# Mixture of experts with a router: slots turned into rows by one-hot products, and gathers and scatters moved into the expert stage

## The reference

```python
xn = (x - mu) * jax.lax.rsqrt(var + EPS) * gamma + beta          # 6250 x 256
logits = jnp.einsum('bsd,de->bse', xn, Wr) + br                  # 8 experts
top_vals, top_idx = jax.lax.top_k(logits, K)                     # K = 2
w = jax.nn.softmax(top_vals, axis=-1)
...
for e in range(E):
    h = jax.nn.gelu(jnp.einsum('bsd,dh->bsh', xn, W1[e]) + b1[e], approximate=False)   # 256 -> 512
    y_e = jnp.einsum('bsh,hd->bsd', h, W2[e]) + b2[e]                                  # 512 -> 256
    y = y + y_e * w_full[..., e, None]
```

## Time and profile before

| | us |
|---|---|
| median of 3 runs | 4773.51 |
| lowest and highest run | 4771.86, 4778.14 |
| the profiled execution | 4775.09 |
| its span, first to last instruction | 4773.1 |

### The profile page before, as it was taken

The page is one execution under the profiler, slowest core; times in us unless marked ns, Lnnn a source line. Parts: engine busy times, 40 slices in busy tenths (PEclk is TensorE's granted clock), DMA queues, the critical chain, the costliest instruction groups (busy, mean ns, idle before and its releaser), DMA issues. The chain is left out here.

```text
span 4773.1 us, 64840 instructions
## 1 busy us (share of the span) xinstructions
PE 3211.2 (67%) x14347; PEld 2378.1 (50%) x14348; DVE 2956.0 (62%) x7184; ACT 2137.5 (45%) x5151; POOL 2786.5 (58%) x2929
## 2 busy tenths in 40 slices
PE   4367777777756677777779477777777450499970
PEld 1255555555545455555569365656565340266640
DVE  5677777777757777777754577777777771022223
ACT  0444434444433344444434477777777450133321
POOL 0277776776657767777746577777777356100016
PEclk9988888888878888888889689898988655699995
DMA  2434333333323333333322111111111613411115
GB/s 85 135 111 116 116 114 109 110 110 110 106 87 109 106 96 109 111 110 110 111 63 72 35 34 35 34 35 34 35 33 33 133 50 124 158 55 55 55 62 144
DMA packets 266610, 411.78 MB, mean 86 GB/s; under 512 B 77798, under 2 KB 183427, under 8 KB 266052
## 3 DMA queue, kind: packets, MB, share of 16 engines
q0 software_dynamic: 120320, 275.83, 22.7%
q1 hardware_dynamic: 145988, 132.65, 8.7%
HBM read 325.12 MB, written 83.11 MB: 86 GB/s over the span
## 5 line engine op out<-in xcount | busy, mean ns | idle before, releaser
L1482 PE MATMUL conv_ps<-conv_msg,conv_S 128*128 128x256 f32 x3328 | 1073.3, 472 | 405.9 <-DVE ACC L1492 310.8
L1482 PEld LDWEIGHTS conv_ps<-conv_msg,conv_S 128*128 128x128 f32 x3328 | 742.3, 236 | 652.7 <-DVE ACC L1492 308.3
L1458 POOL DMA_INDIRECT conv_msg<-relu_xn_table,GI x832 | 787.8, 947 | 387.6 <-issue 247.4
L1458 POOL DMA_INDIRECT conv_msg<-conv_table,GI x832 | 794.5, 955 | 326.5 <-issue 249.6
L2326 POOL DMA_INDIRECT gat_msg<-attn_table,GI x832 | 824.6, 991 | 266.2 <-issue 253.3
L1492 DVE TENSOR_TENSOR ACC<-ACC,conv_ps 128x256 f32 x1664 | 700.7, 421 | 417.1 <-issue 245.7
L1467 ACT ACTIVATE conv_S<-iota_row,LOC 128x128 f32<-128x128 f32 x1664 | 507.3, 388 | 538.2 <-PE conv_ps L1482 529.9
L2383 PE MATMUL gat_ps<-gat_M,gat_S 128*128 128x260 f32 x1664 | 506.7, 458 | 106.4 <-DVE gat_M L2484 102.2
L2383 PEld LDWEIGHTS gat_ps<-gat_M,gat_S 128*128 128x128 f32 x1664 | 364.0, 227 | 185.2 <-DVE gat_M L2484 117.1
L3001 POOL DMA_INDIRECT combine_y<-expert_out,combine_at x98 | 94.1, 960 | 579.7 <-ACTq L2989 559.9
L2441 DVE TENSOR_TENSOR ACC<-ACC,gat_ps 128x260 f32 x832 | 349.0, 419 | 33.9 <-PE gat_ps L2383 11.3
(11 more groups left out here) (535 smaller groups left out, 5625.3 us busy)
## 6 DMA issues: line engine op xcount, KB each, us to landing
expert_in<-heads_zrow SPq DMA_DIRECT2D x53, 256.0 KB
experts_xe<-expert_in SPq DMA_DIRECT2D x106, 128.0 KB
expert_out<-experts_y SPq DMA_DIRECT2D x106, 128.0 KB, 1.7
conv_msg<-relu_xn_table,GI POOLq DMA_INDIRECT x832, 2.8
conv_msg<-conv_table,GI POOLq DMA_INDIRECT x832, 2.8
gat_msg<-attn_table,GI POOLq DMA_INDIRECT x832, 2.5
relu_xn_table<-begin_rx SPq DMA_DIRECT2D x49, 128.0 KB, 1.7
xnT<-begin_xt SPq DMA_DIRECT2D x49, 128.0 KB, 1.8
```

The costliest lines, as they stand in the source:

```text
L1458: pool.indirect_dma_start(self.msg[:, h * RING + k, :], None, table, bass.IndirectOffsetOnAxis(ap=self.m.GI[:, t:t + 1], axis=0)).then_inc ...
L1482: self.nc.tensor.matmul(self.ps[k % self.NB][:, 0:D], self.S[:, r % 2, k, :], self.msg[:, r % self.DEEP * RING + k, :], start=True, stop=T ...
```

## The change

1. **Gamma and beta move behind the transposes.** They are loaded once, at the program's start, as one number per partition (`m.gammac`, `m.betac`, [128, 2]). What PE transposes and SP stores is now the bare `xn`. In heads, ACT's two activations with scale and bias stand where one copy stood, and POOL has nothing to do. In experts, DVE scales the transposed tile with two tensor_scalar operations where ACT copied it.
2. **`expert_in`, its zeros and the dispatch stage are gone.** At the end of route the places are inverted: for each expert tile and slot, which choice (1 to 12,500 and a few) stands there. Each of 98 columns of places gives a one-hot of its slot (`places`, 128 wide) and a one-hot of its tile (`tiles`, 106 wide), which ACT multiplies by the choice's number (`numbered`); PE adds up the 98 products in one PSUM tile. DVE makes them seven columns at a time, 14 rounds, three in flight. A little arithmetic turns the sum into `from_row` (which row of `m.xm` to read) and `to_row` (where in a DRAM tensor `answers` to write).
3. **The experts gather and send.** POOL gathers the 128 rows of each tile from `m.xm` by `from_row` and scatters the answers by `to_row`; SP has no part in the stage. PE's transposes of tile t+1 stand behind tile t's W1 product.
4. **Combine reads plainly.** Answers lie in node order, first all first choices, then all second ones. SP loads them four tiles at a time (two DMAs of 512 KB), DVE does eight operations with one drain, ACT stores 512 KB. Four such parts are in flight, 13 parts in all.
5. **The weights are loaded during route**, from the stage's first moment.

```diff
@@ stage_load
-            for to, frm in ((m.b11s, m.b11), (m.b21s, m.b21)):
+            for to, frm in ((m.b11s, m.b11), (m.b21s, m.b21), (m.gammac, m.gamma), (m.betac, m.beta)):
@@ stage_heads_to_router, scalar
                     if i >= TS:
-                        act.wait_ge(u_made, i - TS + 1)
-                    nc.scalar.activation(t[:, i % TS, :], x_of(i), ACT.Identity, scale=m.rstd[:, i:i + 1],
-                                         bias=shift[:, i:i + 1]).then_inc(t_made, 1)
+                        act.wait_ge(turned, i - TS + 1)
+                        act.wait_ge(out_xn[i % TS], i // TS * 16)
+                    nc.scalar.activation(xn[:, i % TS, :], x_of(i), ACT.Identity, scale=m.rstd[:, i:i + 1],
+                                         bias=shift[:, i:i + 1]).then_inc(xn_made, 1)
...
-                    nc.scalar.copy(xt[:, i % TS, :], pt[i % 2][:, 0:D]).then_inc(xt_made, 1)
+                    for c in range(2):
+                        op = nc.scalar.activation(xt[:, i % TS, c * P:c * P + P], pt[i % 2][:, c * P:c * P + P], ACT.Identity,
+                                                  scale=m.gammac[:, c:c + 1], bias=m.betac[:, c:c + 1])
+                    op.then_inc(xt_made, 1)
@@ stage_route, vector
+            for g in range(CHOICES // SEVEN):
+                if g >= RINGS:
+                    v.wait_ge(placed, g - RINGS + 1)
+                for hot, frm, w in ((places, low, P), (tiles, high, EX_TILES)):
+                    op = nc.vector.tensor_tensor(hot[:, g % RINGS, :, :], m.iota_row[:, 0:w].unsqueeze(1).broadcast_to([P, SEVEN, w]),
+                                                 frm[:, g * SEVEN:(g + 1) * SEVEN].unsqueeze(2).broadcast_to([P, SEVEN, w]), ALU.is_equal)
+                op.then_inc(one_hots, 1)
@@ stage_route, scalar and tensor
+                for k in range(SEVEN):
+                    n = g * SEVEN + k
+                    op = nc.scalar.activation(numbered[:, g % RINGS, k, :], tiles[:, g % RINGS, k, :], ACT.Copy, scale=number[:, n:n + 1])
+                op.then_inc(numbers, 1)
...
+                for k in range(SEVEN):
+                    n = g * SEVEN + k
+                    mm = nc.tensor.matmul(inverse[:, 0:EX_TILES], places[:, g % RINGS, k, :], numbered[:, g % RINGS, k, :],
+                                          start=(n == 0), stop=(n == CHOICES - 1))
+                mm.then_inc(placed, 1)
@@ stage_experts
+        @block.gpsimd
+        def _(pool):
+            for t in range(EX_TILES + BEHIND):
+                if t < EX_TILES:
+                    if t >= 2:
+                        pool.wait_ge(turned, t - 1)
+                    pool.indirect_dma_start(xe[t % 2][:, :], None, m.xm,
+                                            bass.IndirectOffsetOnAxis(ap=m.from_row[:, t:t + 1], axis=0)).then_inc(x_in[t % 2], 16)
+                u = t - BEHIND
+                if u >= 0:
+                    pool.wait_ge(y_made, u + 1)
+                    pool.indirect_dma_start(m.answers, bass.IndirectOffsetOnAxis(ap=m.to_row[:, u:u + 1], axis=0),
+                                            y[u % 2][:, :], None).then_inc(stored[u % 2], 16)
@@ stage_experts, vector
+            def scaled(t, s):
+                v.wait_ge(turned, t + 1)
...
+                for c in range(2):
+                    op = nc.vector.tensor_scalar(xt[s][:, c * P:c * P + P], pt[s][:, c * P:c * P + P], m.gammac[:, c:c + 1],
+                                                 m.betac[:, c:c + 1], ALU.mult, ALU.add)
+                op.then_inc(xt_made, 1)
@@ stage_combine, sync
+            for j, (lo, n, rows) in enumerate(parts):
+                if j >= RINGS:
+                    sp.wait_ge(out_made, j - RINGS + 1)
+                for k in range(2):
+                    sp.dma_start(y[j % RINGS][0:rows, k * FOUR:k * FOUR + n, :],
+                                 rows_of(m.answers, k * TILES + lo, n, rows)).then_inc(got[j % RINGS], 16)
```

283 lines of the change are left out of this document (119 added, 164 removed).

## The result

| | before | after |
|---|---|---|
| median | 4775.16 us (4771.86 to 4778.14) | 4515.93 us (4514.64 to 4520.99, 4 runs) |
| profiled execution's span | 4773.1 us | 4519.3 us |
| ratio of the medians | | 0.9459, 95% interval 0.9443 to 0.9476 |

What follows compares the result with a forecast made beforehand. POOL's indirect DMAs were taken to bound dispatch and combine, PE's wait ahead of W1 the experts, stretched DVE operations heads. Terms +1 - 18 - 118.5 - 38.6 - 67.3 = -241.4 gave 4532 us, range 4505 to 4578.

Steps and rivals of the forecast that it cites:

- Start: Program start: two more small loads in SP's list, ahead of the load of x, cost +1 us.
- Heads: Heads stage: POOL's 98 operations and DVE's stretching go, ACT is late next; -18 us, ends -5 and -25.
- 65.5 + 15 = 81 us: Heads: ACT's busy time plus 15 us for two activations over 35 tiles, as ACT's floor; 82 taken for 100.2.
- Route and dispatch: Last place to experts' start: 158.3 us go, 39.8 us of inversion, small steps and barrier come; -118.5 us.
- The rule on the clock: Inversion on TensorE: small idle gaps make its clock swing, so rounds would cost between 35 and 52 us.
- Experts: Expert stage: period 4.756 to 4.37 us over 106 tiles, -41, ends dearer by 0.8 and 1.5; sum -38.6 us.
- rival A: Experts: the loop through bias and Gelu keeps the period at 4.756 us; 4573 us in all, chance 0.14.
- Combine: Combine stage: plain loads replace 98 gathers and small copies, 69 us for 136.3; -67.3 us, ends -78 and -54.
- B: TensorE stays at 1.2 GHz in the inversion, or combine's DMAs run at 282 GB/s; +17, +13, both 4562; chance 0.13.
- E: Weights written during route slow DVE and still end the stage, or heads gains nothing; 4555 us, chance 0.06.
- C: Experts: POOL's loop sets the pace once gathers land in 4.6 us or more; 4578 at 5.5; chance 0.05.
- D: Experts: same POOL loop with landings over 9.2 us in every tile, slower than before; 4816 at 10; chance 0.02.

Runs made afterwards that it cites:

- e1_pool_busy: Kernel after, with POOL given two operations per tile in heads on tiles of its own that nobody waits for; 4526.94 us, ratio 0.9489.
- e9_late_weights: Kernel after, with SP asking for the experts' weights only when the last inversion product is done; 4540.27 us, ratio 0.9517.
- the two by two: Table of transposes in the product's own step or a step ahead, ACT copying or DVE scaling: 4.756, 5.136, 4.332, 4.327 us a tile.
- e4_behind2: Kernel after with BEHIND = 2, each gather behind the scatter of the tile three before instead of four; 4919.88 us in a single run.
- e2_old_order: Kernel after, with PE's transposes back in the step of their product and DVE's scaling back ahead of that step's bias; 4741.99 us, ratio 0.9944.
- e2b_pe_order: Kernel after, with only PE's transposes back in the step of their product, DVE's list unchanged; 4594.27 us in a single run.
- e10_best: Kernel after, with experts and combine merged, router weights folded and 14 unread warm products on PE in route; 4497.57 us, ratio 0.9425.

## Why the prediction was right, and where it was off

**Start** (+1): right that it is nothing; the +5.6 of the first trace is not the change's.

**Heads** (-18, measured -27.8). The mechanism held: POOL's operations stretched DVE's, ACT is late next. The two activations were priced right. Where ACT waits for nothing, the timeline of the kernel before has a tile's work in 1.37 us:

```profile
3837.29 0.58 ACT L2604 ACTIVATE heads_t<-X,heads_shift,rstd 128x256 f32<-128x256 f32 x1
...
3838.66 0.59 ACT L2604 ACTIVATE heads_t<-X,heads_shift,rstd 128x256 f32<-128x256 f32 x1
```

and that of the kernel after in 1.79, +0.42 for the +0.44 of the prediction:

```profile
3836.38 0.41 ACT L2582 ACTIVATE heads_low<-heads_o 128x256 f32<-128x256 f32 x1
...
3838.17 0.41 ACT L2582 ACTIVATE heads_low<-heads_o 128x256 f32<-128x256 f32 x1
```

The step that failed is the floor, "65.5 + 15 = 81 us". ACT's busy time before was made of operations that each stood out in full ahead of a wait. Back to back they overlap by 0.1 us or so, and the same work takes less. In the same 35 tiles ACT is busy 78.17 us where it was 67.83, +10.3 and not +15. A busy time full of waits was taken as a floor, and it is an upper bound. The second mis-sized term is the end, "0 to -2": it gave 3.7 by the edge at the last statistics. There too POOL had its two operations a tile (busy 18.03 of 23 us), in the chain ahead of the transposes, and the prediction priced only PE. With POOL busy beside it in e1_pool_busy the 3.7 did not come back, so nothing points to the stretching there; the cause stays open.

**Route and dispatch** (-118.5, measured -120.4). Right in its parts: rounds of 33 us for 35, the clock rising within the rounds, ACT then the pace. It rose sooner than the three rounds of the forecast: 0.89 already in 3945 to 3950, with the first product at 3941.84. The rule on the clock that was weighed against it did not show: with short gaps PE stayed at 1.00 from 3950 on. Nor does, which was said to agree with it, bear on it: PE had no short gaps there but had stood idle 3.86 us just ahead.

```profile
254.15 3.27 PE L1482 MATMUL conv_ps<-conv_msg,conv_S 128*128 128x256 f32 x8 [3.86 <-DMA conv_msg<-relu_xn_table,GI]
```

And e9_late_weights confirms the cover, 30 us of it, which the prediction put at 29.

**Experts** (-38.6, measured -35.6). The period is 4.327 where 4.37 was taken, 106 x 0.429 = -45.5. Its reason, that the product no longer waits for `xt`, is confirmed by the two by two. The loop through bias and Gelu that rival A feared does not bind: PE is busy 398.5 of 400 us, PE itself is the bound now. But 9 us go again at the end, because the barrier waits for POOL's drain behind its last scatter. "+1.5 for the last scatter" priced its landing (2.4 us, right) and not the drain of 8.38 us behind it. The kernel before had a place where it could be read (2627.17 to 2638.52). The period came out 4.5 us cheaper than its term and the end dearer, so that the stage as a whole is nearer to the forecast than either.

**Combine** (-67.3, measured -75.6). The shape was right: DMA share over 1, DVE waiting for loads. The rate was not: 347 GB/s, taken from the first load of x, is 385 here, so 19.3 MB take 50 us, not 55. The first part took 5.4 us to land where 3 was taken. From there to the last pair of operations it is 49.1 us, where the prediction had the 55 and 5 more for the last part. DVE did wait 2.99 us for that part, but within the 49.1.

**The rivals.** A, B and E did not occur. C and D need a gather that lands in over 4 us (not 4.6, by the estimate under e4_behind2); no wait for `xe` shows in the 400 us of the stage. E's fear that the weights slow route is refuted.

**The range** held. Of the terms of the sum only the experts' end came out dearer than forecast; heads, combine, the inversion and the period all came out cheaper, heads and combine by 8 to 10 us each. The misses partly cancel: the experts' end alone was 7.6 us dearer, and without that the forecast would have stood that much further off.

## What to carry to other kernels

A stage whose last GpSimd DMAs are scatters to DRAM paid some 9 us at its barrier here that the data do not need, 8.4 of them GpSimd's drain (a stage that ended on seven gathers paid 0.6): let the last scatter be waited for by its consumer inside one stage, or put other work behind it. An engine's drain is not in its busy time; look at the barrier's own line. Before moving work between engines, put a whole step between producer and consumer on the bound engine; after that the engine hardly matters (0.005 us a tile here), before it everything that stands ahead in the new engine's list counts (1.2 us a tile between e2_old_order and e2b_pe_order). And a busy time read from an engine that often waits is more than the same work costs back to back.

## What the runs showed of the hardware

- POOL's drain at a barrier behind scatters to DRAM that have landed: 8.38, 8.22 and 8.06 us at three stage ends, against 0.62 us behind seven gathers. From the last scatter's start to the next stage it is 11.7 and 11.35 us, and 2.5 us where no barrier stood.
- Plain reads and writes of 512 KB moved 385 GB/s in combine, the weights and their broadcasts 381 to 434 GB/s in windows of 5 us (e9_late_weights), against the 347 of the first load of x. The Trainium skill (HBM Reference, "Specifications (TRN2)") gives about 358 GB/s as a core's share and says that a core that streams alone measures about 425. The 385 lies between the two, and the highest of these windows, 434, agrees with the second.
- TensorE's granted clock went from 0.50 (3940 to 3945, the first product at 3941.84) to 1.00 from 3950 on, stayed there through gaps of some 0.25 us between groups of products (PE busy 4.63 of 5 us), and in e10_best was at 0.50 again in 3920 to 3925, where PE had been idle since 3916.7.
- DVE operations of 128x256 with two SBUF inputs took 0.41 to 0.43 us with POOL idle and up to 0.87 beside a POOL operation; with one input they took 0.41 to 0.43 in both cases (e1_pool_busy).
